# Two conditioned attention layers over 32 samples: film products with the weights streamed, bias rows summed on TensorE, small work moved off VectorE, and all queues reordered

## The chip, the cores and the metric

The kernel runs on one core of a Trainium2 chip. The metric is the device time of one execution in microseconds (us). TensorE (PE) multiplies matrices, VectorE (DVE), ScalarE (ACT) and GpSimd (POOL) work elementwise, and SyncE (SP) issues the transfers (DMA). Each engine takes its instructions strictly in its own order and waits on semaphores.

## The reference

The input x has 32 samples of 256 tokens with 256 features; each sample has a condition of 512 values, and two masks. Two layers follow one another, each adding its result to its input:

```
# layer 0, 8 heads of 32              # layer 1, 16 heads of 16
xn = LN(x)                            xn = LN(x)
q = softmax_features(xn@Wq + bq)      q = xn@q_w + q_b
k = softmax_tokens(xn@Wk + bk + mask) k = xn@k_w + k_b
v = (xn@Wv + bv) * mask               v = (xn@v_w + v_b) * mask
y = q @ (k^T v)                       y = softmax(q k^T + (1-mask)*-1e6) v
# both layers
scale, shift = split(silu(cond) @ W_emb + b_emb)          # 512 -> 2*256
h = LN(y) * (1 + scale) + shift
x = x + silu(h) @ W_out + b_out
```

All is float32 outside; inside, weights and activations of the large products are split into a high and a low f16 part, and three f16 products replace one f32 product.

## The kernel before

Once per launch there is a **setup**. It loads the weights raw (`wraw` for q, k, v of both layers, `worw` for the output weights, `wemb0` and `wemb1`, 512x512 each, for film), finds the largest weights (`w0m`, `w1m`, `o0m`, ...), brings the maxima onto all partitions by a transpose and a product on PE (`tr_w0`, `ar_w0`, ...), turns them into powers of two (`w0p`, `w1p`, ...), and splits the weights: the high part on ACT (`wh_k0`, ...), the low part on DVE (`wl_k0`, ...). The norm's bias goes through the weights into a row: `row0` to `row3` are products of one column with a raw weight matrix; `fr0` to `fr2` add the projection's own bias on DVE; `bb0` to `bb2` spread the sum onto 128 partitions with a product against ones; `bc0` to `bc2` copy it to SBUF. The bias of layer 0's k (`row3`, `p3`) is split into three bf16 parts, which a transfer (`aug_d`) puts into rows of `augs`; `k0` adds them by an extra product. The biases of layer 1's q and k are wanted on partitions in a permuted order: `perm` copies the weights and biases permuted (into `XB1` and `prow`), `col` multiplies, and `bm`, `fcs` scale. The conditions are activated (`th`, `csl`), transposed (`cnd`, `csT`), and `fm0`, `fm1` (function `film`) multiply them: for each layer 4 x 4 products of a 128x128 block of weights, loaded, with 32 columns of conditions, moved. `mb0` and `mb1` split the masks of the layers into three parts, `mbd0` and `mbd1` write them to DRAM, from where `am(b)` and `rk6(b)` read one sample's rows. `fill_q0` to `fill_k1` write constants into half of `SQ` and `SK`.

Then each of the 32 samples b passes through **pieces**: layer 0 is `s0` `r0` `z0` (norm: statistics on DVE, root and normalised f16 parts on POOL), `z0T` (transposed by DMA), `k0` `km` `ke` `ktT` `kt`, `q0` `q1` `qm` `qs` `qe` `qtT` `qt`, `v0` `v`, `att` `at` `y0` `Y0`, `s1` `r1` `yn0` `y0T` (second norm), `th0` `st0` `sh0` `sl0` (film and silu), `o0` `x1`; layer 1 is `s2` `r2` `z1` `z1T`, `q1p` `qa` `spq`, `k1p` `ka` `spk`, `v1p` `vt` `vm`, the transfers `wq` `wk` `rq6` `rk6` to DRAM and back, `rows` and `max` (row maxima of the scores, 8 units), `np` and the transfers `nT` `nw` `nr`, `cols`, `exp`, `pv` (scores, exponential, values, 8 units), `yt` `ty` `Y1`, the norm `s3` `r3` `yn1` `y1T`, `th1` `st1` `sh1` `sl1`, `o1`, `o`, and `out_`. `xb0` and `xb1` add the output bias to the residual on POOL; `x_in(b)` loads a sample and waits until `xb0(b - 2)` has freed the buffer.

The order in each engine's queue is written out by hand as a list of calls, setup steps and pieces mixed, several samples deep; `BANK` says which PSUM bank a piece uses for each sample and `FREED` which earlier piece must have read the bank. `SETUP` counts the setup steps of each engine on one semaphore; `ready(e, name)` waits for one of them.

Lines: DVE's bias sums L1357, low parts L1345, `p3_` L1443 to L1450, masks L1362 to L1369, `csT` L1479, norm statistics L1148; PE's `bias_row` L930, `film` L973, `col` L990 and L991, tokens-major f16 products L688; POOL's `xb0` L1947, norm parts L1921, L1925, L1928.

Of the kernel before, what the change touches and what calls it, by code (L numbers as in the profile page):

```python
# [13 lines left out]
P = 128  # L14
# [24 lines left out]
    "gv1": "34002673574122457027061353704073",
    "gr0": "42446426466446426644662046460240",  # L40
    "gr1": "66200002022060240060004420266402",
    "gr2": "06266246644646624646622066406240",
    "gr3": "22662460062620244044262404246206",
    "gr4": "66264006264402424066446660460440",
    "gr5": "02602062024466226004004264606626",
    "gr6": "24260204024200440646460242222400",
    "gr7": "66402422266626626024044662606646",
    "gc0": "62662424266466220460662600042246",
    "gc1": "46422060020022464222446402246024",
    "gpv0": "01377447500341722507275100543515",  # L50
    "gc2": "22044624066266646224602424624242",
    "gc3": "64424062626006002022426044260666",
    "gpv1": "06527021420217352225631215460414",
    "gc4": "22002244264602446442226426626620",
    "gc5": "64244662466066420602064020042442",
    "gpv2": "42466530536301243344061373406552",
    "gc6": "44042246642442660466626400246266",
    "gc7": "60240006242424626020462046262220",
    "gpv3": "02063474032406133161242662517023",
    "gty0": "03167551114007671412204662307110",  # L60
# [2053 lines left out]
```

## Time and profile before

| | before |
|---|---|
| median of 3 runs | 878.3 us (876.21 to 880.64) |
| the profiled execution | 878.06 us, span of its instructions 876.2 us |
| PE busy | 827.4 us, 94% |
| DVE busy | 792.1 us, 90% |
| POOL busy | 725.7 us, 83% |
| ACT busy | 708.0 us, 81% |
| mean granted TensorE clock | 0.971 |

The span runs from the first to the last instruction; the profiled execution took 1.9 us more. Busy time leaves out waits on semaphores. The granted clock is a share of 2.4 GHz. Idle time of an engine that is not the bottleneck costs nothing.

### The profile page before, as it was taken

What the parts mean: (1) busy time and instruction counts of PE and PEld (TensorE: products, weight loads), DVE (VectorE), ACT (ScalarE), POOL (GpSimd) and SP (SyncE); (2) the same over time, 40 slices, a digit from 0 to 9 for tenths busy, and PEclk for the clock granted to TensorE, in tenths of its full rate; (3) what the DMA queues carried; (4) which work ended last, traced back from release to release, by engine and by line L of the source; (5) the groups of instructions that cost most, each with busy time, mean ns of one, the idle gap of its engine ahead of it and who ended that gap; (6) DMA issues with size and microseconds to landing.
All of it is one profiled execution on the core that took longest, in us unless ns stands there. A gap on an engine that the chain in (4) does not pass through costs nothing.

```text
span 876.2 us, 25220 instructions
## 1 busy us (share of the span) xinstructions
PE 827.4 (94%) x8651; PEld 603.3 (69%) x8651; DVE 792.1 (90%) x1633; ACT 708.0 (81%) x1253; POOL 725.7 (83%) x1205
## 2 busy tenths in 40 slices
PE   5997889999999999999999999999999999999885
PEld 2986766667777767777677777777777776656443
DVE  7999799999999999999999999999999999997952
ACT  8744638897898788889788888988988888989794
POOL 7458899889899988988989999998999887977314
PEclk9598999999999999999999999999999999999997
DMA  7211443444255334444352433444454343344211
GB/s 230 68 38 33 117 98 92 106 102 109 49 126 133 98 91 115 91 116 110 81 129 57 137 91 102 96 108 116 118 109 89 74 114 91 95 126 113 74 43 37
DMA packets 149306, 85.84 MB, mean 98 GB/s; under 512 B 87478, under 2 KB 141852, under 8 KB 149180
## 3 DMA queue, kind: packets, MB, share of 16 engines
q1 hardware_dynamic: 149180, 84.23, 39.1%
q8 instruction: 71, 1.16, 0.6%
q14 instruction: 55, 0.45, 0.2%
HBM read 39.52 MB, written 25.79 MB: 75 GB/s over the span
## 4 chain that ended last, share of the span: by engine, by line
PE 39%; POOL 19%; DVE 14%; issue 11%; ACT 5%; DMA 0%; SPq 0%; POOLq 0%; DVEq 0%; ACTq 0%
PE banks L688 11%; PE banks L835 7%; DVE NM L1247 4%; PE banks L696 4%; PE banks L822 4%; PE banks L811 4%; POOL ZHL L1928 3%; PE banks L703 3%; POOL Z L1921 3%; DVE st L1148 2%; PE banks L845 2%; POOL YN L1912 2%; POOL SH L1966 2%; POOL ZHL L1925 2%; POOL AB L1994 2%
## 5 line engine op out<-in xcount | busy, mean ns | idle before, releaser
L1247 DVE TENSOR_REDUCE NM<-banks 128x4 f32<-128x1024 f32 x256 | 302.6, 1212 | 12.2 <-PE banks L811 11.6
L1714 ACT ACTIVATE wraw<-banks,uu 128x1024 f32<-128x1024 f32 x154 | 170.2, 1136 | 22.0 <-PE banks L822 21.4
L1714 ACT ACTIVATE PX<-banks,uu 128x1024 f32<-128x1024 f32 x102 | 112.9, 1138 | 11.4 <-PE banks L822 9.9
L688 PE MATMUL banks<-wo,SH 128*128 128x256 f16 x768 | 96.7, 278 | 5.2 <-POOL SH L1966 4.3
L1908 POOL TENSOR_TENSOR rs<-ve,nhalf 128x2 f32<-128x2 f32 x128 | 91.0, 711 | 10.6
L688 PE MATMUL banks<-wv,ZT 128*128 128x256 f16 x768 | 98.6, 280 | 0.9 <-DVE NM L1247 0.8
L811 PE MATMUL banks<-SK,SQ 51*128 51x256 f16 x1024 | 89.3, 273 | 8.0 <-DVE NM L1247 3.9
L1966 POOL TENSOR_TENSOR SH<-ST,SH 128x512 f16<-128x512 f32 x64 | 73.8, 1158 | 26.1 <-ACT SH L1682 26.1
L1696 ACT ACTIVATE R<-banks,fcs,sqs 128x256 f32<-128x256 f32 x128 | 73.5, 574 | 26.7 <-PE banks L696 20.3
L822 PE MATMUL banks<-SQ,SK 53*128 53x256 f16 x1024 | 90.0, 272 | 5.0 <-ACT wemb L1722 1.3
L1928 POOL TENSOR_TENSOR ZHL<-Z,ZHL 128x256 f16<-128x256 f32 x128 | 87.8, 706 | 5.3
L688 PEld LDWEIGHTS banks<-wo,SH 128*128 128x128 f16 x768 | 73.4, 99 | 23.1 <-POOL SH L1966 9.1
L688 PEld LDWEIGHTS banks<-wv,ZT 128*128 128x128 f16 x768 | 74.8, 100 | 17.3 <-issue 7.5
L835 PE MATMUL banks<-wraw,V 128*32 128x256 f32 x1232 | 85.1, 385 | 1.6 <-ACT wraw L1714 0.6
L1994 POOL TENSOR_TENSOR AB<-R,AB 128x512 f16<-128x512 f32 x64 | 74.5, 1166 | 6.0 <-ACT AB L1696 5.7
L1669 ACT ACTIVATE TH<-banks,hB,hA 128x256 f32<-128x256 f32 x128 | 66.2, 580 | 15.7 <-PE banks L703 14.2
L1921 POOL TENSOR_SCALAR Z<-X,nm,rs 128x256 f32<-128x256 f32 x128 | 74.5, 588 | 3.6 <-POOL ZHL L1928 0.5
L1912 POOL TENSOR_SCALAR YN<-Y,nm,rs 128x256 f32<-128x256 f32 x128 | 72.7, 575 | 2.5
L1696 ACT ACTIVATE AB<-banks,fcs,sqs 128x256 f16<-128x256 f32 x128 | 74.0, 578 | 0.0
L811 PEld LDWEIGHTS banks<-SK,SQ 51*128 51x128 f16 x1024 | 39.1, 94 | 47.6 <-issue 25.3
L822 PEld LDWEIGHTS banks<-SQ,SK 53*128 53x128 f16 x1024 | 38.1, 94 | 45.8 <-issue 27.2
L1906 POOL TENSOR_SCALAR nm<-mv 128x2 f32<-128x2 f32 x128 | 29.0, 226 | 49.0 <-DVE mv L1151 48.2
(180 smaller groups left out, 1971.5 us busy)
## 6 DMA issues: line engine op xcount, KB each, us to landing
scr<-AB SPq DMA_DIRECT2D x64, 256.0 KB, 2.5
X<-in_x_dram SPq DMA_DIRECT2D x32, 256.0 KB, 2.8
SQ<-scr SPq DMA_DIRECT2D x64, 128.0 KB, 2.6
SK<-scr SPq DMA_DIRECT2D x64, 128.0 KB, 2.8
out_dram<-wemb SPq DMA_DIRECT2D x32, 256.0 KB, 2.5
SQ<-scr SPq DMA_DIRECT2D x64, 64.0 KB, 2.7
SK<-scr SPq DMA_DIRECT2D x64, 64.0 KB, 2.9
wemb<-in_L_cond_emb_w_dram SPq DMA_DIRECT2D x1, 1024.0 KB, 5.3
```

Of the source, the lines that this page charges most:

```text
L688: m = PE.matmul(dst[:, t, :], zt[:, j, k, t * P:(t + 1) * P], w[:, i, k, :], start=(k, n) == (0, 0), stop=(k, n) == (1, 2))
L811: m = PE.matmul(banks[:, n + j % 2, (j // 2) * T:(j // 2) * T + T], SQ[p, r, h, c * P:(c + 1) * P], SK[p, r, h, :], start=True, stop=True)
L822: m = PE.matmul(banks[:, n + j % 2, (j // 2) * T:(j // 2) * T + T], SK[p, r, h, c * P:(c + 1) * P], SQ[p, r, h, :], start=True, stop=True)
L835: m = PE.matmul(banks[32 * j:32 * j + 32, n, 0:T], V1[:, r, c, 4 * g + j, :], px((8 * b + u) % 5)[:, at_px(j):at_px(j) + T], start=(c == 0 ...
L1247: V.tensor_reduce(NMe[:, c, :, 2 * g:2 * g + 2], banks[:, n:n + 2, :].rearrange("p a (h m) -> p a h m", m=T), AX.X, ALU.max, negate=True). ...
L1696: t = A.activation(dst, bank(home(f"g{c}1", b))[:, f, :], ACT.Identity, bias=fcs[:, i, f:f + 1], scale=sqs[:, i:i + 1])
L1714: A.activation(px(v % 5), banks[:, n:n + 2, :].rearrange("p a n -> p (a n)"), ACT.Exp, scale=uu[:, 0:1]).then_inc(S["exp"])
L1908: G.tensor_tensor(rs[:, b % 2, l, :], ve[:, l, :], nhalf[:, :], ALU.pow).then_inc(S[f"r{l}"])
L1921: i = G.tensor_scalar(Z[:, t, :], src[:, t, :], nm[:, b % 2, 2 * l, t:t + 1], rs[:, b % 2, 2 * l, t:t + 1], ALU.add, ALU.mult)
L1928: i = G.tensor_tensor(h[:, 1, k], z[:, :, k, :], h[:, 0, k], ALU.subtract)
L1966: G.tensor_tensor(SH[:, l, 1], ST[:, l], SH[:, l, 0], ALU.subtract).then_inc(S[f"sl{l}"])
L1994: G.tensor_tensor(AB[:, i, :, 1], R1[:, i], AB[:, i, :, 0], ALU.subtract).then_inc(S["sp" + c])
```

## The change

- **Film**: the conditions are now the operand that is loaded (128x32), and the weights stream past them, 512 columns at a time (`cond_rows`, steps `fx0` `fx1`, 4 products a layer). The result, 32 rows of 512, is copied by ACT into the first rows of `wemb` (`fy0`, `fy1`) and transposed by 4 small transposes a layer (`fm0`, `fm1`).
- **Biases**: `bias_all` loads the norm's bias broadcast to 128 columns, so that the sum comes out on all partitions at once, and adds the projection's bias by a third product; `row0` to `row2` and `fr0` to `fr2` are gone. `row3` adds its bias by a third product too. For layer 1's q and k, `rw` makes the bias rows with 6 products, `perm` copies two rows permuted, and `col` has 4 products of one row instead of 12; the permuted copies of the weights are gone, and with them `xb1(0)`'s wait for `col`.
- **Off DVE**: the three parts of k's bias go ACT, POOL, ACT, POOL, ACT (`pa`, `pb`, `pc`, `pd`, `p3`), `mc` and `csT` to ACT, `mb1` to POOL. The permuted high and low parts of layer 1's q and k take one instruction for a block of 256 columns instead of two of 128.
- **Order**: the queues of all five engines, `BANK`, `FREED` and `SETUP` are written anew, for the whole run. On SP `ld_o0` stands ahead of `ld_r`, `mbd0` behind both film loads, `ld_o1` behind `am(1)`. On ACT `fill_q1` stands between `qt(4)` and `kt(4)`. On POOL `pb` and `pd` stand ahead of `z0(2)`, `v1z` behind `r0(3)`, `mb1` behind `yn0(2)`. On DVE `o1m` and `mx_o1` stand behind the first `s1`.

```diff
-            def bias_row(i, l, w):
+            def row3():
+                e.wait_ge(l_w[0], 80)
+                e.wait_ge(l_row, 96)
+                ready(e, "cst")
+                clear(e, "grow3", 0)
+                for k in range(2):
+                    PE.matmul(at_row(3)[0:1, :], lnc[:, 0, 1, k:k + 1], wraw[:, 1, k, :], start=(k == 0), stop=False)
+                PE.matmul(at_row(3)[0:1, :], one1[0:1, 0:1], brow[:, 3, :], start=False, stop=True).then_inc(C["PE"])
+
+            def bias_all(i, l, w):
+
                 e.wait_ge(l_w[l], 80)
-                clear(e, f"grow{i}", 0)
+                e.wait_ge(l_row, 96)
+                ready(e, "cst")
+                clear(e, f"gbb{i}", 0)
                 for k in range(2):
-                    m = PE.matmul(at_row(i)[0:1, :], lnc[:, l, 1, k:k + 1], wraw[:, 3 * l + w, k, :],
-                                  start=(k == 0), stop=(k == 1))
-                m.then_inc(C["PE"])
-
-            def bias_all(i):
-                ready(e, f"fr{i}", "cst")
-                clear(e, f"gbb{i}", 0)
-                PE.matmul(at_all(i), ones3[0:1, :], frow[:, i, :], start=True, stop=True).then_inc(C["PE"])
...
+                    PE.matmul(at_all(i), lnc[:, l, 1, k:k + 1].to_broadcast([P, P]), wraw[:, 3 * l + w, k, :],
+                              start=(k == 0), stop=False)
+                PE.matmul(at_all(i), ones3[0:1, :], brow[:, i, :], start=False, stop=True).then_inc(C["PE"])
...
-            def film(l):
+            def cond_rows(l):
+
                 ready(e, "csT")
                 e.wait_ge(l_f[l], 64)
+                clear(e, f"gfx{l}", 0)
+                for k in range(4):
+                    t = PE.matmul(at_conds(l), csT[:, k, :], wemb[l][:, k, :], start=(k == 0), stop=(k == 3))
+                t.then_inc(C["PE"])
+
+            def film(l):
+                ready(e, f"fy{l}", "cst")
                 clear(e, f"gfm{l}", 0)
                 for m in range(4):
-                    for k in range(4):
-                        t = PE.matmul(at_film(l, m), wemb[l][:, k, m * P:(m + 1) * P], csT[:, k, :],
-                                      start=(k == 0), stop=(k == 3))
+                    t = PE.transpose(at_film(l, m), wemb[l][0:NB, 0, m * P:(m + 1) * P], ident[0:NB, 0:NB])
                 t.then_inc(C["PE"])
...
+            def rw():
+
+                e.wait_ge(l_w[1], 80)
+                e.wait_ge(l_row, 96)
+                ready(e, "cst")
+                clear(e, "grw", 0)
+                for i in range(2):
+                    for k in range(2):
+                        PE.matmul(at_rows(i), lnc[:, 1, 1, k:k + 1], wraw[:, 3 + i, k, :], start=(k == 0), stop=False)
+                    t = PE.matmul(at_rows(i), one1[0:1, 0:1], brow1[:, i, :], start=False, stop=True)
+                t.then_inc(C["PE"])
+
             def col():
-                ready(e, "perm")
+                ready(e, "perm", "cst")
                 clear(e, "gcol", 0)
                 for i in range(2):
                     for f in range(2):
-                        o, cc = at_col(2 * i + f), slice(f * P, (f + 1) * P)
-                        for k in range(2):
-                            PE.matmul(o, XB1[:, i, k, cc], lnc[:, 1, 1, k:k + 1], start=(k == 0), stop=False)
-                        t = PE.matmul(o, prow[:, i, cc], one1[0:1, 0:1], start=False, stop=True)
+                        t = PE.matmul(at_col(2 * i + f), prow[:, i, f * P:(f + 1) * P], one1[0:1, 0:1], start=True, stop=True)
...
@@ DVE, low_part (ACT's high_part is changed in the same way) @@
                     if swap:
-                        o, h = (v_.rearrange("p (e f h) -> p e f h", e=2, f=16) for v_ in (o, h))
-                        r = r.rearrange("p (h e f) -> p e f h", e=2, f=16)
-                    for f in range(2) if swap else (slice(None),):
-                        t = V.scalar_tensor_tensor(out=o[:, f], in0=r[:, f], scalar=sl[:, l, i, k:k + 1], in1=h[:, f],
-                                                   op0=ALU.mult, op1=ALU.subtract)
+                        o, h = (v_.rearrange("p (g h) -> p g h", h=8) for v_ in (o, h))
+                        r = r.rearrange("p (h g) -> p g h", h=8)
+                    t = V.scalar_tensor_tensor(out=o, in0=r, scalar=sl[:, l, i, k:k + 1], in1=h, op0=ALU.mult, op1=ALU.subtract)
...
@@ ACT, new @@
+            def pa():
+                ready(e, "row3", "w0p", "cst")
+                for o in (frow[:, 3, :], p3[:, 0, :]):
+                    A.activation(o, at_row(3)[0:1, :], ACT.Identity, scale=iu[0:1, 1:2])
+                A.activation(augs[0:6, :], augs[0:6, :], ACT.Identity, scale=iu[0:6, 1:2]).then_inc(C["ACT"])
...
+            def conds(l):
+
+                ready(e, f"fx{l}")
+                A.activation(wemb[l][0:NB, 0, :], at_conds(l), ACT.Identity).then_inc(C["ACT"])
...
@@ POOL, new @@
+            def mb1():
+                def part(n):
+                    return G.tensor_scalar(mh3[:, n, :], mbf[:, 1, :], 1.0, 0.0, ALU.mult, ALU.add)
+
+                def rest(n):
+                    return G.tensor_tensor(mbf[:, 1, :], mbf[:, 1, :], mh3[:, n, :], ALU.subtract)
+
+                e.wait_ge(l_msk, 32)
+                ready(e, "fcs")
+                follow(G.tensor_scalar(mbf[:, 1, :], mrow[:, 1, :], -1.0, NEG, ALU.add, ALU.mult))
+                follow(G.tensor_scalar(mbf[:, 1, :], mbf[:, 1, :], tm[0:NB, :], 1.0, ALU.mult, ALU.mult))
+                follow(part(0))
+                follow(rest(0))
+                follow(part(1))
+                follow(rest(1))
+                part(2).then_inc(C["POOL"])
+
+            def pb():
+
+                ready(e, "pa")
+                G.tensor_tensor(left[:, 0, :], frow[:, 3, :], p3[:, 0, :], ALU.subtract).then_inc(C["POOL"])
...
@@ SP, the first calls @@
-            ld_m(); ld_c(); x_in(0); x_in(1); ld_w1(); x_in(2); ld_w0(); mbd0(); ld_r(); ld_f1(); ld_o1(); am(0)
-            ld_f0(); ld_o0(); x_in(3); x_in(4); z0T(0); aug_d(); am(1); am(2); am(3); z0T(1); z0T(2); am(4)
...
+            x_in(0); ld_c(); ld_m(); x_in(1); ld_w1(); x_in(2); ld_w0(); ld_o0(); ld_r(); ld_f1(); ld_f0(); mbd0()
+            x_in(3); x_in(4); am(0); am(1); ld_o1(); z0T(0); am(2); z0T(1); aug_d(); z0T(2); z0T(3); am(3); am(4)
...
@@ PE, the first calls @@
-            cnd_t(); pm(); row2(); row1(); tr_w1(); row0(); row3(); bb2(); tr_w0(); bb1(); ar_w1(); bb0(); ar_w0()
-            fm1(); fm0(); k0(0); v0(0); tr_o0(); col(); tr_f0(); q0(0); ar_o0(); v0(1); ar_f0(); tr_o1(); ktT(0)
...
+            pm(); tr_w1(); bb0(); cnd_t(); tr_w0(); ar_w1(); row3(); ar_w0(); bb2(); fx1(); tr_o0(); fx0()
+            ar_o0(); fm1(); rw(); q0(0); fm0(); bb1(); k0(0); v0(0); tr_f0(); q0(1); k0(1); ktT(0); v0(1); v0(2)
...
```

## Rows read from the trace of the kernel before

**Rows 1.** The page: share of the span busy; TensorE's granted clock in 40 slices.

```profile
PE 827.4 (94%) x8651; PEld 603.3 (69%) x8651; DVE 792.1 (90%) x1633; ACT 708.0 (81%) x1253; POOL 725.7 (83%) x1205
...
PEclk9598999999999999999999999999999999999997
```

**Rows 2.** Windows: stretch, length, busy us (instructions) of each engine, clock, DMA.

```profile
10.00:60.00 50.00, 48.52 (x279) 38.78 (x278) 45.66 (x147) 34.04 (x50) 29.60 (x51) 0.76 0.39 102
60.00:100.00 40.00, 33.26 (x265) 28.35 (x264) 35.57 (x100) 20.67 (x49) 33.18 (x53) 0.91 0.25 55
100.00:200.00 100.00, 92.83 (x922) 67.88 (x920) 91.21 (x188) 72.98 (x143) 90.50 (x151) 0.98 0.42 101
200.00:800.00 600.00, 590.72 (x6516) 433.94 (x6518) 567.45 (x1106) 515.65 (x922) 538.13 (x886) 1.00 0.42 103
```

**Rows 3.** Windows of PE alone: busy us, clock, DMA share, GB/s.

```profile
18.00:20.00 2.00, 2.00 (x11) 1.00 0.60 207
22.00:24.00 2.00, 2.00 (x11) 0.50 0.79 192
```

**Rows 4.** PE's instructions in order of time: start, us, what.

```profile
9.65 1.86 PE L930 MATMUL banks<-wraw,lnc 128*1 128x256 f32 x4 [1.79 <-DMA lnc<-in_L_cond_norm_b_dram]
...
15.10 2.79 PE L930 MATMUL banks<-wraw,lnc 128*1 128x256 f32 x8
...
20.05 13.59 PE L973 MATMUL banks<-csT,wemb 128*128 128x32 f32 x64
33.49 1.44 PE L718 MATMUL banks<-ZT,wk 128*128 128x256 f16 x6
...
42.39 2.73 PE L688 MATMUL banks<-wq,ZT 128*128 128x256 f16 x12
...
48.84 1.47 PE L688 MATMUL banks<-wq,ZT 128*128 128x256 f16 x12
```

**Rows 5.** DVE's instructions in order of time.

```profile
8.78 0.26 DVE L1479 TENSOR_SCALAR csT<-banks 128x128 f32<-128x128 f32 x1
...
13.91 0.41 DVE L1357 TENSOR_TENSOR SQ<-banks,SK 1x256 f32<-1x256 f32 x1
...
24.29 1.44 DVE L1345 SCALAR_TENSOR_TENSOR wq<-wraw,sl,wq 128x128 f16<-128x128 f32 x4
25.64 0.40 DVE L1443 TENSOR_TENSOR SQ<-banks,SK 1x256 f32<-1x256 f32 x1
...
27.12 1.36 DVE L1445 TENSOR_SCALAR SQ<-SQ,iu 1x256 f32<-1x256 f32 x1
...
30.26 0.86 DVE L1345 SCALAR_TENSOR_TENSOR wv<-wraw,sl,wv 128x256 f16<-128x256 f32 x2
...
58.15 0.74 DVE L1148 BATCH_NORM_STATS2 st<-Y 128x6 f32<-128x256 f32 x2
...
88.26 0.25 DVE L1362 TENSOR_SCALAR SK<-SK 32x256 f32<-32x256 f32 x1
...
91.81 0.58 DVE L1197 SCALAR_TENSOR_TENSOR AT<-banks,rk,blk 128x128 f32<-128x128 f32 x2
```

**Rows 6.** POOL's and SP's queues in order of time.

```profile
25.85 2.50 POOL L1947 TENSOR_TENSOR XB<-X,bobc 128x512 f32<-128x512 f32 x2 [4.71 <-DMA bobc<-in_L_cond_b_out_dram]
...
28.96 1.34 SPq L521 DMA_TRANSPOSE ZT<-ZHL  x1
```

**Rows 7.** POOL's groups from 0 to 60 us: busy us, mean ns, idle before.

```profile
L1928 POOL TENSOR_TENSOR ZHL<-Z,ZHL 128x256 f16<-128x256 f32 x10 | 6.8, 703 | 0.4
L1921 POOL TENSOR_SCALAR Z<-X,nm,rs 128x256 f32<-128x256 f32 x10 | 5.8, 582 | 0.3 <-POOL ZHL L1928 0.3
L1925 POOL TENSOR_SCALAR ZHL<-Z 128x256 f16<-128x256 f32 x10 | 4.2, 440 | 0.4
```

**Rows 8.** ACT's instructions in order of time.

```profile
32.99 5.32 ACT L1775 ACTIVATE SQ<-one 32x6144 f16<-32x6144 f32 x1
43.18 0.56 ACT L1640 ACTIVATE KE<-banks,km,un 128x256 f32<-128x256 f32 x1 [4.88 <-DVE km L1163]
```

More of the change, by code:

```diff
@@ L39 @@
[L39 to L60, printed above, removed]
@@ L255 @@
+    "ga_b": "mx_b",
+    "gfx0": "w0p",
+    "gfm0": "mc",
+    "gfx1": "mx_w0",
+    "gfm1": "fy1",
 }
@@ L258 @@
     "PE": (
-        "cnd pm row2 row1 tr_w1 row0 row3 bb2 tr_w0 bb1 ar_w1 bb0 ar_w0 fm1 fm0 tr_o0 col tr_f0 ar_o0 ar_f0 "
-        "tr_o1 tr_f1 ar_o1 tr_b ar_b ar_f1 ").split(),
+        "pm tr_w1 bb0 cnd tr_w0 ar_w1 row3 ar_w0 bb2 fx1 tr_o0 fx0 ar_o0 fm1 rw fm0 bb1 tr_f0 ar_f0 col tr_f1 "
+        "tr_o1 ar_o1 tr_b ar_b ar_f1 ").split(),
     "DVE": (
-        "mb0 csl csT w1m fr2 fr1 w0m mx_w1 fr0 mc mx_w0 w1p w0p o1m wl_q1 p3 wl_v0 wl_k0 o0m f1m f0m wl_q0 "
-        "wl_k1 mx_o0 wl_v1 mx_f0 o0p film0 mx_o1 wl_o0 bm mx_b o1p mx_f1 fcs mb1 film1 wl_o1 ").split(),
+        "mb0 csl w1m w0m mx_w1 o0m mx_w0 w1p w0p wl_q1 wl_v1 mx_o0 wl_k0 wl_q0 o0p f1m wl_v0 f0m wl_k1 mx_f0 "
+        "film0 wl_o0 bm o1m mx_o1 mx_b fcs o1p mx_f1 film1 wl_o1 ").split(),
     "ACT": (
-        "th fill_k1 fill_q0 fill_k0 wh_q1 wh_k1 wh_q0 bc0 wh_v0 wh_k0 perm wh_v1 bc1 fill_q1 wh_o0 bc2 wh_o1 ").split(),
+        "th fill_k0 fill_k1 csT bc0 wh_q1 wh_v1 pa wh_k0 wh_q0 pc fy1 p3 wh_v0 mc fy0 fill_q0 perm wh_k1 bc1 "
+        "wh_o0 bc2 fill_q1 wh_o1 ").split(),
     "POOL": (
-        "cst v1z nmz ").split(),
+        "cst pb nmz pd v1z mb1 ").split(),
 }
@@ L1986, in xb1 @@
                     e.wait_ge(l_o[1], 32)
-                first(e, b, "col")
                 G.tensor_tensor(XB1[:, b % 4], X1[:, b % 2], both(bobc[:, 1, :]), ALU.add).then_inc(S["xb1"])
@@ new lines, in _ @@
+            r2(0); xb1(0); z1(0); sl0(1); r0(5); r1(2); z0(5); yn0(2); mb1(); r2(1); spq(0); z1(1); spk(0); sl0(2)
+            xb0(3); xb1(1); qs(5); r1(3); xb0(4); yn0(3); r2(2); spk(1); spq(1); vm(0); r0(6); z1(2); r0(7)
+            sl0(3); z0(6); z0(7); r1(4); xb0(5); r2(3); yn0(4); z1(3); spk(2); spq(2); qs(6); r1(5); vm(1); yn0(5)
+            sl0(4); xb1(2); r0(8); vm(2); qs(7); z0(8); xb0(6); r2(4); spq(3); z1(4); spk(3); sl0(5); xb1(3)
+            r1(6); qs(8); r0(9); z0(9); spk(4); xb0(7); yn0(6); spq(4); r3(0); r2(5); r0(10); yn1(0); z1(5)
```

959 lines of the change are left out of this document (477 added, 482 removed), and 210 rows, old and new, of the table FREED.

## The prediction

> **What bounds the kernel now.** I first read the page's totals and its 40 slices of 21.9 us [rows 1]: TensorE is busy 94% of the span. The reader is to see in the row of its clock the 5 tenths of full speed in the second slice and the 8 in the fourth, in slices where PE is busy. Then the windows [rows 2]: from 200 to 800 us PE is busy 590.7 of 600 us at a granted clock of 1.00. In that stretch only less matmul work or 9.3 us of PE idle time could be gained, and the change takes no matmul out of it. It touches it through the order of the pieces alone. From 60 to 200 us PE idles 6.7 + 7.2 = 13.9 us, with DVE and POOL about as busy as PE. So what the edits themselves are worth is settled in the setup, and the question is how many us earlier the pipeline of 32 samples gets under way, and how much of that lead arrives at 200 us.
>
> The finer clock view [rows 3] and PE's list in order of time [rows 4] explain the slices. The film products, 64 instructions with 128x128 weights and 32 columns moved, take 13.59 us. The clock is 1.00 (2.4 GHz) before them and 0.50 (1.2 GHz) soon after they begin. It is back for a while behind the first dense f16 products, which begin at 33.49, and is lost again with the 24 small instructions of `col`: the 12 f16 products right behind them take 2.73 us, the same 12 at 48.84 us 1.47. PE is at work all the time from 20 to 60 us, but on things worth half of it.
>
> DVE is the other engine without a pause: from 10 to 60 us it is busy 45.7 of 50 us [rows 2]. In its list [rows 5] I see setup work of short, dependent instructions. `p3_` takes eight of them, from 25.64 to the next start at 30.26 us, one of them 1.36 us long on a single partition, beside a POOL instruction that runs 25.85 to 28.35 [rows 6], where the first took 0.40; `mb1` takes seven, 3.5 us from 88.26 on. ACT in contrast waits 4.88 us for DVE's `km` before its first `ke` [rows 8].
>
> **The change part by part, DVE.** Taken off before the first `s1` (58.15 us): csT 0.26 and `mc`, a copy of the same shape, 0.26, three bias sums 3 x 0.41 = 1.2, `p3_` 25.64 to the next start at 30.26 = 4.6 [rows 5]. The swapped low parts become two instructions of 256 strided elements where four of 128 took 1.44 us: two plain ones of 256 took 0.86, so each weight saves between 0 (strided elements cost twice) and 0.6; I take 0.25, the middle, twice: 0.5. Sum 6.8 us. Besides, `o1m` and `mx_o1` (some 1.2 us by the shapes of theirs that stay) are moved behind the first `s1`: the lead there is 8.0, and these 1.2 are paid back later. Of the 4.3 us in which DVE waited between 10 and 60 us I expect 1 to go, since bias rows, `csT` and `p3` hand-overs no longer pass through it.
>
> **TensorE.** It must not hold that lead up. A f32 product of 256 columns is two instructions, 0.43 us apart at 1.2 GHz (the first `bias_row` group, 4 in 1.86 us; the clock column reads 1.00 there, but eight later ones take 2.79 us, so the engine sped up within them) and 0.21 at 2.4 GHz by half. New: three `bias_all` of 3 products, `row3` 3, `rw` 6, so 18 products, 7.7 us fast or 15.5 slow; the two `cond_rows` 8 products of 512 columns, 6.8 us or 13.7; eight small transposes some 1.2. `col` keeps 4 of 12 products, a third of the 3.9 us between the f16 groups. Gone: 11 products of 256 columns and the 13.6 us of film. The film edit at 1.2 GHz is thus worth nothing (13.7 against 13.59). Its worth hangs on the clock, and here the row speaks for the change: the `bias_row` streams ahead of film got faster while they ran, the weight-bound film lost it [rows 3, 4]. I take the high level from about 17 us on.
>
> The order: PE starts streaming when the bias rows have landed. DVE read them at 13.91 us [rows 5]; ahead of `ld_r` SP now issues two DMAs of `ld_o0` in place of the one of `mbd0`, so about 14.4. From there 3 x 1.3 + 0.6 (`cnd_t`) + 1.5 (transposes and spreads of the maxima, my estimate) + 6.8 + 0.6 (`fm1`) + 2.6 (`rw`) = 16.0, with 1.5 for the slow start and 1.5 for waits on `w0p`: `q0(0)` at about 33.4, `k0(0)` at 36.8 behind `fm0` and `bb1`, `q0(1)` done near 41.5. Before, `k0(0)` began at 33.49, but `q0(1)` ended at 50.3 [rows 4]. So PE is 9 us ahead there and DVE's 8 is what counts.
>
> **Queues.** SP's `x_in(3)` stood behind `xb0(0)`, which waited until 25.85 us for a bias of `ld_o0`; the first transpose was issued at 28.96 [rows 6]; `k0(0)` could not begin before it had landed, some 3 us later. With `ld_o0` ahead of 2 MB of film weights this wait goes. What is late next is `mbd`: written behind `ld_f0` now, and `am(0)`, which waits for it, stands ahead of `z0T(0)`. I put it at 23 us and the transpose, behind `ld_o1`, at 25: ready by 28, before `q0(0)`. `aug_d` waits for ACT-POOL-ACT-POOL-ACT (`pa` to `p3`) behind `w0p` and goes out by 28, landing near 31, before `k0(0)`. On POOL `pb` and `pd` hold `z0(2)` until about 27, and `v1z`, a memset of some 3 us, moves from the front to there: both lie in POOL's idle time, of which the 4.71 us ahead of `xb0(0)` are one piece [rows 6]. ACT loses eight permuted copies and the fill and gains some ten short activations: less than before, and its wait of 4.88 us covers the rest.
>
> **After the start.** `mb1` leaves DVE (3.5 us, on the chain of waits of before) for POOL. By nearest rows on POOL [rows 7]: two TENSOR_SCALAR 0.58, three with f16 out 0.44, two TENSOR_TENSOR 0.70 = 3.9 us. It stands ahead of `spq(0)`, `z1(1)` and `spk(0)`, which the first `rows` wait for. POOL has 16.3 us idle in 60 to 200 us [rows 2], so it costs 0 to 3.9; DVE gives 0 to 3.5. I take both whole, +0.4. The Trainium skill speaks against this move: GPSIMD Engine Reference, section Engine selection, gives elementwise work to VectorE and calls GpSimd about 2x slower for two inputs. The rows have 0.41 us on DVE and 0.70 on POOL for 256 elements a partition, 1.7 times. By the rule the two subtractions would be 1.6 instead of 1.4 us, 0.2 more.
>
> `fill_q1`, 5.32 us, ran where ACT had nothing to do; now it stands between `qt(4)` and `kt(4)`, with `qa(1)`, `ka(1)`, `ke(5)` queued behind it and `rq6(0)` waiting for it. ACT is idle 19.3 of the 40 us from 60 to 100 [rows 2]. Cost 0 to 5.3, I take 1.
>
> **Sum.** -8.0 -1.0 +1.2 +0.4 +1.0 = -6.4 us; the order of the long middle I take at zero, between -9.3 (no PE idle left) and, by the same size, +9.3. The profiled execution took 878.06 us, the median of the runs is 878.3. I say 872 us; own range 867 to 876.
>
> **Rivals.** (1) The lead is lost on the way to 200 us: POOL takes `mb1` in full, DVE's saving is no help, and `fill_q1` holds ACT: -6.8 + 3.9 + 2.5 = about 878. For it: POOL is 90.5% busy from 100 to 200 us and much of the chain runs over it; against: both blocks meet idle time. 0.20. (2) The clock does not rise in the streams, or is lost at once: PE adds 7.7 + 6.9 = 14.6 us to the 41.5, `q0(1)` ends at 56, 5.8 us later than before, and the time is 884. It decides when more than some 9 us of streaming run at 1.2 GHz. For it: the first streams ran slow, and only one column of weights was loaded in those that sped up; against: the later ones were fast. 0.07. (3) The new order costs PE waits in the middle: idle doubles, -6.4 + 9.3 = 881. For it: every queue is reordered and nothing in the trace favours either. 0.12. (4) PE's work counts instead of DVE's: film 13.6, `col` 2.6 and half the time of the slow f16 groups, 4.2, less streams of 6.8 + 1.2 + 3.0, are 9.4 us, and the middle gives up half of its 9.3 of idle: -14, 864. For it: PE is the bound from 200 us on; against: DVE has no slack to follow it. 0.11. The forecast keeps 0.50.
>
> **How the numbers follow.** What can be told from no change is 0.5%, 4.4 us: below 873.9 or above 882.7. Faster: 0.50 x 0.8 + 0.11 + a tenth of rivals 1 and 3 = 0.56. Slower: rival 2, and a third of rival 3, 0.11. Same: 0.33. The range is 864 to 881: rival 2 and the ends of 3 and 4 are left out, under 2 in 10.
>
> **What would show it.** DVE's first `s1` near 50 us instead of 58.15; `cond_rows` at some 0.43 us an instruction with the clock at 1.00 from 20 us on; no 1.1 us instructions on 6 partitions on DVE; PE 200 to 800 us busy as before. I am wrong if the streams take 0.86 us each, if ACT's fill is followed by PE idle at 80 to 90 us, or if PE's idle time in the middle moves by more than 5 us.

## The result, and the profile after

The changed kernel takes 876.71 us (median of 20 runs, 873.36 to 879.27), the kernel before 879.11 (20 runs beside it). The ratio is 0.997, 95% interval 0.9955 to 0.9984: a gain of 0.3%, some 2.5 us, where 6.4 were forecast. It is below the 0.5% that the prediction took as the limit of what can be told from no change. The profiled execution took 876.07 us, its span is 873.8 (before: 876.2). Two executions of the experiments below lie far off all others (2732 us in e0, and the profiled one of e12, 1585 us), and the ratios leave them out.

The page of the changed kernel, the rows that answer to [rows 1]:

```profile
PE 820.7 (94%) x8609; PEld 589.1 (67%) x8609; DVE 782.1 (90%) x1609; ACT 710.8 (81%) x1250; POOL 734.8 (84%) x1214
...
PEclk9998999999999999999999999999999999999998
```

The windows, answering to [rows 2] (stretch, length, busy us and instructions of each engine, clock, DMA share, GB/s):

```profile
10.00:60.00 50.00, 45.95 (x256) 28.59 (x257) 41.73 (x133) 30.50 (x51) 31.66 (x52) 1.00 0.41 107
60.00:100.00 40.00, 34.83 (x273) 29.54 (x271) 30.31 (x90) 24.61 (x45) 35.82 (x59) 0.91 0.22 52
100.00:200.00 100.00, 91.68 (x918) 67.72 (x918) 94.24 (x190) 75.06 (x145) 91.15 (x151) 0.98 0.42 99
200.00:800.00 600.00, 589.39 (x6498) 431.41 (x6499) 563.92 (x1105) 516.38 (x922) 538.83 (x884) 1.00 0.42 102
```

DVE now idles 8.3 us of the 50 from 10 to 60 us, where it idled 4.3; I had expected a microsecond less, not four more. The long middle is as before. TensorE's list in order of time, answering to [rows 4] (start, us, what), says what DVE waits for:

```profile
14.05 0.38 PE L864 MATMUL banks<-ident,mxw 128*3 128x128 f32 x1 [8.10 <-DMA SK<-in_L_cond_k_b_dram]
14.30 2.04 PE L941 MATMUL banks<-wraw,lnc 128*128 128x256 f32 x4
...
18.62 1.86 PE L931 MATMUL banks<-wraw,lnc 128*1 128x256 f32 x4
...
21.86 2.08 PE L941 MATMUL banks<-wraw,lnc 128*128 128x256 f32 x4
...
25.02 5.35 PE L967 MATMUL banks<-wemb,csT 128*32 128x512 f32 x8
30.30 0.27 PE L864 MATMUL banks<-ident,mxw 128*1 128x128 f32 x1
30.50 3.62 PE L967 MATMUL banks<-wemb,csT 128*32 128x512 f32 x8
...
37.58 1.48 PE L687 MATMUL banks<-wq,ZT 128*128 128x256 f16 x12
```

`bb0` starts at 14.30, as forecast (14.4). But its four instructions of 256 columns take 2.04 us, `row3`'s 1.86 and `bb2`'s 2.08, 0.5 us each: the low rate. The two `cond_rows` are the same eight instructions each, and take 5.35 us and 3.62. One by one, those of the first start at 25.02, 25.87, 26.72, 27.58, 28.43, 28.91, 29.34 and 29.77: 0.85 us apart up to 28.43, 0.43 from there on. So TensorE worked from 14.05 to 28.43 us at 1.2 GHz. The clock column does not say so:

```profile
18.00:20.00 2.00, 2.00 (x7) 1.00 1.03 379
22.00:24.00 2.00, 2.00 (x5) 1.00 0.41 138
```

These windows of PE answer to [rows 3]. They read 1.00 in a stretch where the instructions take nearly twice what they take at the high rate (`row3` 1.86 us here, 1.02 in e4 below). In this profile the column is no evidence ahead of the first fall that it shows; the durations are.

`q0(0)` starts at 37.58 instead of 33.4, `k0(0)` at 41.04 instead of 36.8. DVE's list, answering to [rows 5], shows the wait for PE and the first `s1`:

```profile
30.60 0.28 DVE L1304 TENSOR_REDUCE mxc<-banks 1x1 f32<-1x128 f32 x1 [4.17 <-PE banks L864]
...
35.31 1.68 DVE L1380 TENSOR_SCALAR be1c<-bec 128x2 f32<-128x2 f32 x1
...
55.28 0.74 DVE L1164 BATCH_NORM_STATS2 st<-Y 128x6 f32<-128x256 f32 x2
```

The first `s1` is 2.9 us earlier than before, not 8. The queues of SP and POOL, answering to [rows 6, 7], did what the prediction said of `z0T(0)` (25) and `mb1` (3.9 us, 83.67 to the next start at 87.57); `aug_d` went out at 31.32 instead of by 28, still ahead of `k0(0)`:

```profile
25.31 1.35 SPq L520 DMA_TRANSPOSE ZT<-ZHL  x1
```

```profile
83.67 0.40 POOL L2042 TENSOR_SCALAR SK<-SK 32x256 f32<-32x256 f32 x1
...
87.57 0.18 POOL L1903 TENSOR_SCALAR nm<-mv 128x2 f32<-128x2 f32 x1
```

ACT, answering to [rows 8]: its wait is now in front of `ke(4)`, and `fill_q1` stands at 92.92.

```profile
83.99 0.56 ACT L1607 ACTIVATE KE<-banks,km,un 128x256 f32<-128x256 f32 x1 [6.81 <-DVE rk L1183]
...
92.92 5.32 ACT L1772 ACTIVATE SQ<-one 32x6144 f16<-32x6144 f32 x1
```

Three marks split the 2.4 us between the spans. First `s1`: 58.15 before, 55.28 after, 2.9 ahead. First `max`: 111.65 and 111.22, 0.4 ahead, so the stretch between the two grew from 53.5 to 55.9. End of the span: 2.4 ahead. The first `max` before and after:

```profile
111.65 2.35 DVE L1247 TENSOR_REDUCE NM<-banks 128x4 f32<-128x1024 f32 x2
```

```profile
111.22 2.32 DVE L1263 TENSOR_REDUCE NM<-banks 128x4 f32<-128x1024 f32 x2
```

### The profile page after: what moved, and what is told of

Read it like the earlier page. It is cut to its first block, busy times and chain, and to the rows that moved or that the text cites. A ratio compares the mean times of both kernels' runs of the same rounds, so it can differ in the third digit from the quotient of the medians.

```text
span 873.8 us, 25110 instructions
## 1 busy us (share of the span) xinstructions
PE 820.7 (94%) x8609; PEld 589.1 (67%) x8609; DVE 782.1 (90%) x1609; ACT 710.8 (81%) x1250; POOL 734.8 (84%) x1214
## 4 chain that ended last, share of the span: by engine, by line
PE 40%; POOL 23%; DVE 17%; issue 11%; ACT 3%; DMA 3%; SPq 2%; POOLq 0%; DVEq 0%; ACTq 0%
PE banks L687 11%; DVE NM L1263 7%; PE banks L834 5%; PE banks L695 4%; PE banks L821 3%; POOL Z L1918 3%; PE banks L810 3%; PE banks L717 3%; POOL AB L1989 3%; POOL ZHL L1925 3%; DVE st L1164 3%; PE banks L702 3%; POOL SH L1963 2%; POOL rs L1905 2%; DMA ZT<-ZHL 2%
## 5 line engine op out<-in xcount | busy, mean ns | idle before, releaser
L687 PE MATMUL banks<-wv,ZT 128*128 128x256 f16 x768 | 95.9, 276 | 0.1
L687 PEld LDWEIGHTS banks<-wv,ZT 128*128 128x128 f16 x768 | 74.0, 99 | 14.6 <-issue 5.8
L1918 POOL TENSOR_SCALAR Z<-X,nm,rs 128x256 f32<-128x256 f32 x128 | 76.7, 606 | 4.1 <-issue 1.3
L1909 POOL TENSOR_SCALAR YN<-Y,nm,rs 128x256 f32<-128x256 f32 x128 | 70.9, 561 | 2.6
L1639 ACT ACTIVATE HH<-banks,fB,fA 128x256 f32<-128x256 f32 x128 | 66.6, 588 | 0.0
```

What stands on the lines that cost most here:

```text
L687: m = PE.matmul(dst[:, t, :], zt[:, j, k, t * P:(t + 1) * P], w[:, i, k, :], start=(k, n) == (0, 0), stop=(k, n) == (1, 2))
L1918: i = G.tensor_scalar(Z[:, t, :], src[:, t, :], nm[:, b % 2, 2 * l, t:t + 1], rs[:, b % 2, 2 * l, t:t + 1], ALU.add, ALU.mult)
```

## The experiments

All kernels but e12 are edits of the changed kernel. The kernel before ran beside each group of them: 877.99 us (29 runs) for e0 to e3, 877.81 (17) for e4 to e7, 878.18 (23) for e8 to e11, 878.67 (23) for e12 to e14. Ratios are to it.

**Is it the rate?** e1 adds six products that nobody reads in TensorE's empty 8 us:

```diff
+def fast_early():
+    for k in range(6):
+        PE.matmul(banks[:, 6, :], ident[:, :], ident[:, :].unsqueeze(1).to_broadcast([P, 4, P]), start=True, stop=True)
-pm(); tr_w1(); bb0(); ...
+pm(); fast_early(); tr_w1(); bb0(); ...
```

> The changed kernel with six f32 products of 512 columns that nobody reads (128x128 identity as weights, the identity four times as columns, into a bank that is free until the first att), put behind pm, where TensorE otherwise waits from 5.9 to 14.1 us. Theory A (the engine's history sets the rate: the streams ran at half rate until 28.4 us because PE came to them from an idle stretch): the rate rises within the added products, bb0's four instructions then take 0.21 us each instead of 0.5, the twelve of cond_rows 0.43 each from the first on, q0(0) starts near 32 us instead of 37.6, DVE's first s1 near 51 instead of 55.3, and the time falls by 2 to 4 us to about 873.5. Theory B (what is lost is lost in 60 to 111 us, whatever the start): the same early times, but the first max stays at 111 us and the time at 876.7. Theory C (the rate hangs on the streams themselves, not on what ran before): the added products may be fast, but bb0 and bb2 are slow again, and nothing moves.

Measured: 873.74 us, ratio 0.9963 (0.9945 to 0.9981). e0 is the changed kernel once more beside it:

> The changed kernel itself, for comparison on the same chip with the three others. All theories: 876 to 877.5, about 2.5 us under the kernel before; q0(0) near 37.6, cond_rows slow until about 28 us if that is a property of the kernel, and at another time if it is a chance of that one execution.

Measured: 876.81 us, 0.9989 (0.9968 to 1.0011); `q0(0)` at 39.13, first `s1` 56.84, and the rise within the first `cond_rows` at 30.86. The low rate up to there belongs to the kernel; the place of the rise moves by 2.4 us between executions. TensorE's list in e1:

```profile
5.86 7.64 PE L927 MATMUL banks<-ident 128*128 128x512 f32 x12
13.56 0.27 PE L864 MATMUL banks<-ident,mxw 128*3 128x128 f32 x1
15.06 1.10 PE L945 MATMUL banks<-wraw,lnc 128*128 128x256 f32 x4 [1.23 <-issue]
...
17.62 1.86 PE L935 MATMUL banks<-wraw,lnc 128*1 128x256 f32 x4
...
24.02 5.30 PE L971 MATMUL banks<-wemb,csT 128*32 128x512 f32 x8
```

Windows of PE in e1:

```profile
16.00:18.00 2.00, 2.00 (x11) 0.80 0.53 88
18.00:20.00 2.00, 2.00 (x6) 0.50 1.02 376
```

The added products start 0.85 us apart up to 10.29 and 0.43 from 10.77 on. `bb0` then takes 1.10 us instead of 2.04: theory C falls. But `row3` is slow again, and now the column shows it, because there is a fall to record. Only `bb0` was won; `q0(0)` is at 36.53, first `s1` at 54.30. So the time is the 873.5 of theory A by luck: the early times that it was to come from are not there in this profile. The twelve executions say more. Three have a mean granted clock of 0.990 to 0.993 and took 871.3 to 871.9 us; nine, the profiled one among them, have 0.982 to 0.986 and took 872.7 to 877.6. A mean near 0.99 alone could also come of a rate that was never reached, but such an execution would take the changed kernel's 876 us. So the same kernel seems to keep the rate in some executions and to lose it in most, and the median is a mixture.

**Keeping the rate.** e4 fills the pause as well, with eight such products:

```diff
-pm(); tr_w1(); bb0(); cnd_t(); tr_w0(); ar_w1(); row3(); ar_w0(); bb2(); fx1(); ...
+pm(); fast(6); tr_w1(); fast(2); bb0(); cnd_t(); tr_w0(); ar_w1(); row3(); ar_w0(); bb2(); fx1(); ...
```

> The changed kernel with eight of the unread products of 512 columns in place of the first experiment's six: six behind pm and two more behind tr_w1, so that TensorE is at work without a pause until bb0's operands are there near 15 us. In the first experiment bb0 ran fast (1.10 us for four instructions) after six, and row3 behind it slow again, with 1.23 us of idle time and 1.6 us of small products in between. Theory A1 (the idle 1.23 us cost the rate): row3 takes 1.02 us for its four, bb2 1.1, cond_rows 3.4 for its first eight, q0(0) near 33 us, first s1 near 51.5, time near 872. Theory A2 (the small products behind bb0, of one row or three rows of weights and of 32 columns, cost the rate): bb0 fast, row3 and bb2 slow again, q0(0) within 0.7 us of the first experiment's 36.53, time near 874.

Measured: 869.65 us, 0.9917 (0.9899 to 0.9936). Repeated later as e14:

> The kernel of e4_early_8 once more, beside the two others on the same chip: 869 to 870.5 us, first s1 within 1 us of 50.4, if the rate is held as there; one of its groups of instructions at half rate behind a pause of TensorE, and a time of 873 to 876, if that is a matter of chance.

Measured: 871.42 us, 0.9901 (0.9868 to 0.9934). The median of the twelve runs of both is 870.45, some 7.8 us under the kernel before. TensorE's and DVE's lists in e4:

```profile
15.45 1.03 PE L945 MATMUL banks<-wraw,lnc 128*128 128x256 f32 x4
...
17.76 1.02 PE L935 MATMUL banks<-wraw,lnc 128*1 128x256 f32 x4
...
19.54 1.13 PE L945 MATMUL banks<-wraw,lnc 128*128 128x256 f32 x4
...
21.23 3.62 PE L971 MATMUL banks<-wemb,csT 128*32 128x512 f32 x8
...
32.06 1.48 PE L687 MATMUL banks<-wq,ZT 128*128 128x256 f16 x12
```

```profile
50.39 0.74 DVE L1168 BATCH_NORM_STATS2 st<-Y 128x6 f32<-128x256 f32 x2
```

Every stream is fast, `q0(0)` starts at 32.06 (forecast 33.4) and the first `s1` at 50.39 (forecast 50): the setup that I had predicted, reached when the one assumption in it is made true (with `bb0` starting at 15.45, 1.1 us later than forecast).

e5 puts two more products among the short ones (`ar_w1(); fast(1); row3(); ar_w0(); fast(1); bb2()`), e6 leaves out of e4 the one-row products that add the biases:

> The kernel of e4_early_8 with one more such product (two instructions, 0.86 us at the high rate, 1.7 at the low) behind ar_w1 and one behind ar_w0, that is among the small products. Theory A2: the rate is held through row3 and bb2, cond_rows fast from the first on; row3 saves 0.8, its one-row product 0.4, bb2 1.5, cond_rows 1.8, the small ones 0.5, so 5.0 less 1.7 for the two products: q0(0) 3 us earlier than with six early ones, near 33.3, time near 871 to 872. Theory A3 (row3 with its single column of weights does not hold the rate whatever stands around it): row3 or bb2 slow again, q0(0) at 37 or later, time no better than e4_early_8.

> The kernel of e4_early_8 without the products of one row by 256 columns that add the bias vectors in bb0, bb1, bb2, row3 and rw (the biases are left out of the computation). Theory A2, with these one-row products as the part that costs the rate: row3 and bb2 fast, q0(0) 33 us less the products' own 5 x 0.6 = 3, near 31 to 32, first s1 near 50, time 870 to 872. If the transposes of 32 columns and the 3-row spreads cost it, or row3: row3 slow as before, q0(0) only 5 x 0.6 to 1.0 earlier than e4_early_8.

Measured: 870.57 us, 0.9921 (0.9906 to 0.9937), and 870.54 us, 0.9921 (0.9906 to 0.9937). In both every stream is fast: `q0(0)` at 34.65 and 30.74, first `s1` at 53.20 and 50.01. Once e4 had the rate there was nothing left to keep. In e6 `q0(0)` is 1.3 us earlier than in e4, but its first `s1` lies between those of e4 and e14 (50.39 and 49.65), and DVE idles only 2.6 us from 10 to 50: with fast streams DVE sets the start. e5 pays for its products at `q0(0)` and at the first `s1`, 2.8 us later than in e4, but not at the first `max` (106.32 against 106.26) and not in the time. Its stretch between the two marks is 53.1 us; the ten other profiles with the same order there have 55.1 to 56.0. It is also the only one in which the clock shows no fall from 55 to 115 us; the windows of PE from 65 to 70 us in e4 and in e5:

```profile
65.00:70.00 5.00, 5.00 (x32) 0.66 0.18 54
```

```profile
65.00:70.00 5.00, 3.12 (x26) 1.00 0.18 52
```

One profile is no proof, and no run tests it. e9 leaves the same products out of the changed kernel, without early ones:

> The changed kernel, no early products, without the one-row products that add the bias vectors (the biases are left out of the computation). In the changed kernel the rate rose at 28.43 us, 3.4 us into cond_rows, though TensorE had worked since 14.05. Theory D1 (the one-row products delay the rise): four-instruction row3 or bb2 are the first fast ones, at 18 to 21 us, cond_rows 0.43 us an instruction from the first on, q0(0) near 32, time near 872. Theory D2 (they do not matter; bb0, row3 and bb2 of 2 us each between short products are too short a stretch, and only cond_rows raises it): the rise again about 3.4 us into cond_rows; PE saves 5 x 0.6 to 1.2 us of product time, q0(0) 34 to 35, time 874 to 876.

Measured: 871.00 us, 0.9903 (0.9877 to 0.9930). `bb0`, `row3` and `bb2` take 2.04, 1.86 and 2.08 us as before, and the rate rises between 26.04 and 26.64, again inside the first `cond_rows`: D2. `q0(0)` is at 34.17, as expected; the time is 3 us better than expected and near theory D1's 872. The marks place the difference only in part: first `s1` at 53.54, first `max` at 109.16, 2.1 us ahead of the changed kernel's profile and 3.5 ahead of e0's, with another 1.7 to 3.1 gained behind it. That rest is not explained. So a time near e4's is no proof of the high rate by itself; the marks of e4 are.

Is it the pause that loses the rate? e1 says so with 1.23 us. But e5, which has two more long products behind it, had one of 1.34 us, at 12.7, and kept it; e6, without them, had 0.82 and 0.69 and kept it; and e13 (below) lost it inside `bb2` with a pause of only 0.35:

```profile
17.56 1.02 PE L935 MATMUL banks<-wraw,lnc 128*1 128x256 f32 x4
...
19.34 1.74 PE L945 MATMUL banks<-wraw,lnc 128*128 128x256 f32 x4
```

What decides in these 8 us of short products stays open, and by the twelve executions of e1 part of it is chance. e8 shows the loss behind a long pause. It moves work in the middle (`fill_q1` on ACT to behind `pc`, `km(4)` and `rk(3)` on DVE ahead of `mx_b`) and was meant for another question:

```diff
-ACT: ... pc(); fy1() ... qt(4); fill_q1(); kt(4)
+ACT: ... pc(); fill_q1(); fy1() ... qt(4); kt(4)
-DVE: s1(2); mx_b(); fcs_(); km(4); rk(3)
+DVE: s1(2); km(4); rk(3); mx_b(); fcs_()
...
```

> The kernel of e4_early_8 (869.65 us) with the middle reordered: fill_q1 on ACT behind pc, and km(4) and rk(3), both, on DVE ahead of mx_b and fcs. In e7_middle km(4) went alone, and ke(4) waited 6.83 us all the same, now for rk(3) behind fcs. Theory B (this wait and the 4.0 us of DVE behind it cost the stretch from first s1 to first max 2.4 us): ke(4) starts 4 to 5 us earlier, the 4.0 us wait on DVE goes, first s1 to first max 53.5 instead of 55.9 us, time 867.5 to 868.5. Theory A alone (DVE's and ACT's idle time there are cover, the stretch is set by POOL, which is busy 49 to 52 of 56 us): the wait moves elsewhere, the stretch stays within 0.7 us, time within 1 us of 869.65.

Measured: 876.04 us, 0.9951 (0.9929 to 0.9974), 5.6 us worse than e4's kernel. TensorE's list:

```profile
25.60 3.62 PE L971 MATMUL banks<-wemb,csT 128*32 128x512 f32 x8
...
32.11 0.60 PE L978 MATMUL banks<-ident,wemb 32*128 32x32 f32 x4 [2.59 <-ACT wemb L1751]
32.65 1.87 PE L1001 MATMUL banks<-wraw,lnc 128*1 128x256 f32 x4
```

I had costed `fill_q1` at nothing behind `pc`, since ACT waits there. With fast streams that cover is gone: `fy1` comes late, TensorE pauses for 2.59 us, and `rw` behind it takes 1.87 instead of 1.02 us for four. `q0(0)` starts at 38.12 instead of 32.06 and the first `s1` at 57.64 instead of 50.39. Pause and lost rate together cost all that e4 had won at the start. Not in every execution: two of the twelve took 869.8 and 870.5 us, with mean clocks of 0.991 and 0.994, the ten others 873.2 to 879.3 with 0.986 to 0.990. The one profile is of the ten.

**What the film edit is worth.** e3 puts the old film form into the changed kernel, e10 into e4:

```diff
-for k in range(4):
-    t = PE.matmul(at_conds(l), csT[:, k, :], wemb[l][:, k, :], start=(k == 0), stop=(k == 3))
+for m in range(4):
+    for k in range(4):
+        t = PE.matmul(at_film(l, m), wemb[l][:, k, m * P:(m + 1) * P], csT[:, k, :], start=(k == 0), stop=(k == 3))
...
```

> The changed kernel with the film products in their old form: per layer 16 f32 products with 128x128 weights and 32 columns in place of 4 products of 512 columns, the copy on ACT and four transposes; mc on ACT goes ahead, as its bank is needed. In the changed kernel the new form takes 5.35 + 3.62 us of PE plus transposes of about 1.2, some 10; the old one took 13.6 in the kernel before, at half rate. Theory A: PE reaches q0(0) about 3.5 us later than 37.6, near 41, s1 later by 2 to 3, time up by 1 to 3 us, to 878 to 880. Theory B (loss in 60 to 111 us whatever the start): start later by as much, but first max near 111 and the time at 876.7. If PE is at the high rate in the old form too (weights reloaded 128 columns for every 32 moved), the form is worth nothing: q0(0) at 37 to 38.

> The kernel of e3_old_film (film in its old form, 882.65 us) with the eight early products of e4_early_8. Theory A (the old form, 128x128 weights loaded for every 32 columns moved, loses the rate, as in the kernel before): bb0, row3 and bb2 fast, film fast at first and then 0.43 us a product as before (some 12 to 13.9 us in all), rw slow behind it, q0(0) near 40 to 42, time near 878. If the old form keeps the rate once it has it: 32 products in some 7 us, like the new form's 7.2, q0(0) near 32, and the time near e4_early_8's 869.65, so that the film edit would be worth nothing at the high rate.

Measured: e3 882.65 us, 1.006 (1.0037 to 1.0084); e10 876.43 us, 0.9974 (0.9952 to 0.9996). Against 876.81 and 870.45 with the new form, that is 5.8 and 6.0 us. TensorE's list in e10:

```profile
21.04 4.17 PE L969 MATMUL banks<-csT,wemb 128*128 128x32 f32 x32
...
25.22 6.87 PE L969 MATMUL banks<-csT,wemb 128*128 128x32 f32 x32
```

The old form starts at the high rate and loses it: the second 32 instructions take 6.87 us, the first 4.17, and `rw` behind them is slow. In e3 it is slow throughout (7.04 and 6.88), `q0(0)` starts at 45.36 and the first `s1` at 64.47, with DVE waiting 5.87, 4.14 and 4.09 us.

**Do early products help the kernel before?** e12:

```diff
-cnd_t(); pm(); row2(); row1(); ...
+cnd_t(); pm(); fast(2); row2(); fast(1); row1(); ...
```

> The kernel before with three of the same unread products: two behind pm and one behind row2, in TensorE's idle stretches of 1.79 and 1.49 us ahead of the bias rows. It asks how much of the 8 us of e4_early_8 belongs to the early products alone. Theory A (film in its old form loses the rate, as the second half of it did in e10_early_8_old_film, and DVE, busy without a pause in the kernel before, sets its start): the rate is high from about 13 us on, the bias rows and the first 32 film products save some 4 us of TensorE, the rest is slow as before; DVE's first s1 moves by less than 1 us from 58.15, the time stays within 1.5 us of 878. Rival (TensorE's rate is the whole gain whatever the form): first s1 near 54 and a time near 874 or less.

Measured: 878.43 us, 0.9996 (0.9974 to 1.0018): nothing. There is no profile of it that can be used, so which part of theory A holds (the film losing the rate, or DVE) is only argued.

**DVE's wait for `tr_o0`.** e2 moves `tr_o0` ahead of `bb2` and `ar_o0` ahead of `fx0`:

> The changed kernel with tr_o0 taken from behind fx1 on PE to ahead of bb2, and ar_o0 from behind fx0 to behind fx1. DVE's wait of 4.17 us at 26.4 goes: mx_o0 can start at 26.4, wl_k0 and wl_q0 end near 29.5 instead of 33.5. Theory D (the order of DVE's work behind tr_o0 holds the start up): DVE's first s1 comes 2 to 4 us earlier and q0(0) up to 3 us earlier. Theory A (PE's slow streams hold it up): PE reaches q0(0) at 37.6 as before, since it runs almost without a pause up to there; DVE's idle time only moves to 33 to 38 us, first s1 within 1 us of 55.3, time within 1 us of 876.7.

Measured: 876.07 us, 0.9974 (0.9959 to 0.9990), 0.7 from e0. The 4.17 us are gone, a wait of 2.99 us for `fm1` has come at 34.99, first `s1` is at 55.54: DVE waits for TensorE's streams, wherever the wait stands.

**The stretch from the first `s1` to the first `max`.** e7 has `fill_q1` behind `pc` and `km(4)` ahead of `mx_b` without early products; e13 is e4 with `km(4)`, `rk(3)` moved and `th0(2)` on ACT ahead of `kt(3)` and `qa(0)`; e11 is e4 with `mb1` on DVE behind `fcs`:

> The changed kernel with two pieces moved and nothing else: fill_q1 on ACT from between qt(4) and kt(4) to behind pc, where ACT waits 3.58 us for fx1, and km(4) on DVE from behind fcs to ahead of mx_b, so that ke(4) on ACT does not wait 6.81 us and st0(2) not 4.01 us behind it. From the first s1 to the first max the changed kernel takes 55.9 us, the kernel before 53.5. Theory B (2.4 us are lost there by the order): the wait of 4.01 us on DVE goes, s1 to max 53 to 54 us, first max near 109, time down by 1 to 2 us. Theory A alone (only the start matters; DVE's idle time there is cover): first max within 0.7 us of 111.2 and the time within 1 us of the changed kernel's.

> The kernel of e4_early_8 with km(4) and rk(3) on DVE ahead of mx_b and fcs and, on ACT, th0(2) ahead of kt(3) and qa(0). In e8_early_8_middle ke(4) got ahead of fcs, but qa(0), which reads fcs and stands ahead of th0(2), waited for it, so that st0(2) waited 4.72 us. Theory B (this wait is where the stretch from the first s1 to the first max is 2.4 us longer than before): the wait is gone or under 1 us, first s1 to first max 53.5 to 54.5 us, time 867.5 to 868.5. Rival (POOL, busy 52 of 56 us there, or PE sets the stretch): the stretch 55.4 to 56 us again, time within 1 us of 869.65.

> The kernel of e4_early_8 with mb1 back on DVE, behind fcs and ahead of km(4), as in the kernel before. The prediction priced the move at +0.4 us (3.9 on POOL against 3.5 on DVE). If POOL sets the stretch up to the first max: z1(1) and spk(0) some 3.9 us earlier, first max 1 to 3 us earlier than e4_early_8's 106.26, time 867 to 868.5. If DVE sets it: km(4), rk(3), ke(4) 3.5 us later, first max 1 to 3 us later, time 871 to 873. If both have slack there: within 1 us of 869.65.

Measured: e7 875.32 us, 0.9981 (0.9965 to 0.9996), the stretch 55.4 us, DVE's wait 4.66 instead of 4.0. e13 876.00 us, 0.9977 (0.9953 to 1.0001), the stretch 61.3 us in a profile of its slowest execution (880.93): DVE still waits 3.85, and 5.98 more for `att` at 94.78. e8's stretch was 55.4. Moving single pieces did not win the 2.4 us. With `th0(2)` ahead of `qa(0)` the copies that a product of TensorE waits for come late; it pauses for 4.67 us, and behind the pause it is at the low rate again, six f16 products in 1.44 us that take 0.81 in e4:

```profile
89.89 1.44 PE L717 MATMUL banks<-ZT,wk 128*128 128x256 f16 x6 [4.67 <-ACT AB L1667]
```

```profile
90.00:94.00 4.00, 4.00 (x20) 0.50 0.25 70
```

So the move opened a pause of TensorE where e4 has one of 0.63 us. e11 871.31 us, 0.9909 (0.9882 to 0.9936): its stretch is 57.8 against 55.9 in e4 and 56.0 in e14, so `mb1` on POOL seems worth 1.8 us at the first `max`, by one profile; between the times (871.31 against 870.45) nothing can be told. On DVE its seven instructions take 2.6 us here, from 78.02 to the next start at 80.58, not the 3.5 of [rows 5]: the second subtraction took 1.31 us there and takes 0.41 here.

## Why the prediction was wrong

By its own sum: -8.0 and -1.0 at the start, +1.2, +0.4 and +1.0 on the way, the middle 0.

- **"I take the high level from about 17 us on" is the step that failed.** It was 28.43 us (30.86 in e0). The prediction added 16.0 us of fast products, 1.5 for a slow start and 1.5 for waits on `w0p`; the row shows 23.3 us from 14.30 to 37.58, without a wait. e4 takes 16.6 us for the same groups at the high rate. So the low rate cost 6.7: `bb0`, `row3` and `bb2` with their one-row products 1.5, 1.3 and 1.5, the first `cond_rows` 1.7, the small products 0.7. Of that 1.5 were booked, and 1.5 more were free, as the waits did not come; with the 0.6 by which 16.0 was short, that is the 4.2 that `q0(0)` is late. The reasoning behind it was a row where the rate rose inside a longer run of like products (16.77, in the third `bias_row` group), carried over to streams cut up by short ones; and a clock column that I read as true ahead of the first fall. e4 makes the assumption true, with eight products that compute nothing, and gets the forecast start and a time of 870.45.
- **DVE's 8.0 and the 1.0 of waits.** The work did leave DVE: it is busy 41.7 us of 50 instead of 45.7. But it turned into idle time, 8.3 us instead of 4.3, most of it for TensorE (4.17 and 1.25 us). The lead at the first `s1` was 2.9 (1.3 in e0). With fast streams it was 7.8 and 8.5. So the size was right and its condition was not. The sentence "PE is 9 us ahead there and DVE's 8 is what counts" compared the engines at `q0(1)`, which ended 4.9 us ahead, and not where DVE waits: at `tr_o0`, behind the first `cond_rows`. From the start of `tr_o0` to the first `s1` it is 25.0 us here, in e0 and in e1 alike, and in this profile DVE idles only 1.0 us of them behind its wait, so each slow stream ahead of `tr_o0` is paid in full.
- **`v1z` at nothing.** The prediction put this memset into POOL's idle time. It runs from 34.31 to 36.97 us, and in it a DVE instruction that takes 0.16 us elsewhere takes 1.68 and ends with it (last section). How much of that reaches the first `s1` no run shows: in e0 nothing is stretched, and the first `s1` still comes 25.0 us after `tr_o0`.
- **+1.2, +0.4, +1.0.** Together 2.6; the stretch in which they fall grew by 2.4. That the sum agrees does not show each: `mb1`, booked at +0.4, was a gain of 1.8 at the first `max` by e11's one profile; `fill_q1`, together with `km(4)`, was worth at most 0.5 by e7 (55.4 against 55.9). What fills the rest in that stretch (the place of `fcs`, the waits behind it, falls of the clock) is not settled; e5 passed it in 53.1 us with the same order.
- **The middle at zero.** From the first `max` to the end the changed order gained 2.0 us here; over the 15 profiles of kernels with that order of the middle, fast start or slow, it is 0.6 to 4.8, mean 2.5, each against the one profile of before. The interval given for it, -9.3 to +9.3, holds that; if that one profile is typical, the value taken was some 2 us too pessimistic, and that hid part of the failed step.
- **The film edit** was priced by its condition, "worth nothing at 1.2 GHz". It was worth 5.8 us in a kernel whose streams ran half of the time at 1.2 GHz, because the rate rose inside the new form's products and was high for what followed, while in the old form it stayed low (e3) or fell (e10).
- **The rivals.** Rival 2 named the mechanism and priced it at 884: it let all streams and everything up to `q0(1)` run slow. The rate came back at 28.43, which left 6.7 of its 14.6 us; and it let PE's loss count only beyond 9 us, which the wait at `tr_o0` does not bear out. Rival 1's 878 is near the time for another reason: the lead was not lost on the way, it was not there. The chance for "no change" was 0.33 (the chances given for "faster" add up to 0.54, not 0.56, which would make it 0.35). The range of 864 to 881 held the time, the forecast's own of 867 to 876 missed it by 0.7.

The Trainium skill's rule on VectorE against GpSimd (GPSIMD Engine Reference, section Engine selection) would have kept `mb1` on DVE. Its factor of about 2 is for two inputs: the two subtractions take 0.67 and 0.66 us on POOL and 0.41 each on DVE (e11), 1.6 times. All seven instructions take 3.9 and 2.6 us, 1.5 times; by e11's profile the move paid all the same at the first `max`.

## What to carry to other kernels

A move of work to TensorE should be priced at both of its rates, and the rate at the start of a kernel read from durations of like instructions, not from a clock column that has not yet shown a change. If TensorE comes to a chain of short products from an idle stretch, products that nobody reads, put where it has nothing to do, can be the cheapest edit there is: eight of them were worth 6.4 us here (876.81 to 870.45), more than twice the whole change. Three of them in the kernel before were worth nothing. And the gain holds only as long as no later wait opens a pause: in e8, whose profile shows one of 2.59 us, most or all of it was gone in ten of twelve executions. When two kernels differ in such a way, look at the mean clock of every execution and not at one profile alone.
